# Aggregation of a graph attention layer: how far one-hot matrices are made ahead, and where they are kept

## The reference

```
z = einsum('ni,hoi->nho', h, Wfc)           # 3750 x 8 heads x 64
alpha = ex / denom[dst]                     # one coefficient per edge and head
msg = alpha[:, :, None] * z[src]
out = segment_sum(msg, dst, num_segments=N) # sum over the edges of each node
```

## Time and profile before

| | |
|---|---|
| median of 3 runs | 3725.33 us |
| profiled execution: time, span | 3727.02 us, 3724.9 us |
| TensorE, weight loads | busy 2880.1 us (77%), 1386.2 us |
| VectorE, ScalarE, GpSimd | 2141.4 us, 611.7 us, 1619.3 us |
| mean granted TensorE clock | 0.88 of full speed |
| aggregation of layer 0 | 529 to 1158 us of the span |
| aggregation of layer 1 | 2549 to 3179 us |

### The profile page before, as it was taken

One profiled execution on the slowest core, in us unless ns is written; L12 is line 12 of the kernel. 1 busy time (PEld: TensorE's weight loads), 2 busy tenths in 40 slices (PEclk: granted clock), 3 DMA queues, 4 the chain that ended last, 5 costly groups with the idle time before them and its releaser, 6 DMA issues. The chain is left out here.

```text
span 3724.9 us, 37926 instructions
## 1 busy us (share of the span) xinstructions
PE 2880.1 (77%) x9194; PEld 1386.2 (37%) x9195; DVE 2141.4 (57%) x3396; ACT 611.7 (16%) x1083; POOL 1619.3 (43%) x1595
## 2 busy tenths in 40 slices
PE   5988638988886881499998598925988887649980
PEld 2444312222223551255553244512223322546660
DVE  5779786666654876633331404587666664754445
ACT  2100110000003650011111210012111110611110
POOL 0777027777760000144443077404777775002216
PEclk9999869999997875699999799967999998559995
DMA  4336227777761211055554537404777775143337
GB/s 155 87 98 117 87 63 211 210 210 211 210 190 52 77 68 68 21 138 144 142 141 99 145 89 160 128 7 126 211 210 211 210 211 150 73 165 127 126 104 249
DMA packets 330788, 512.22 MB, mean 138 GB/s; under 512 B 172499, under 2 KB 178115, under 8 KB 329999
## 3 DMA queue, kind: packets, MB, share of 16 engines
q0 software_dynamic: 113824, 311.79, 31.4%
q1 hardware_dynamic: 92975, 194.62, 14.9%
q10 hardware_dynamic: 123840, 3.94, 1.9%
HBM read 423.29 MB, written 86.92 MB: 137 GB/s over the span
## 5 line engine op out<-in xcount | busy, mean ns | idle before, releaser
L1049 PE MATMUL bank<-aggregate_zg,aggregate_onehot 128*128 x2112 | 1085.9, 640 | 167.0 <-DVE aggregate_zg L1019 95.0
L976 POOL DMA_INDIRECT aggregate_zg<-z_rows,src_groups x940 | 889.1, 946 | 657.1 <-POOLq L2239 334.9
L1019 DVE TENSOR_TENSOR aggregate_zg<-aggregate_zg,bank 128x1024 f32<-128x1024 f32 x470 | 573.9, 1221 | 467.6 <-DMA aggregate_zg<-z_rows,src_groups 467.1
L1049 PEld LDWEIGHTS bank<-aggregate_zg,aggregate_onehot 128*128 128x128 f32 x2112 | 348.4, 193 | 903.2 <-issue 896.8
L376 POOL DMA_INDIRECT front_d<-src_scores,src_chunks x320 | 321.5, 1005 | 188.6 <-issue 97.2
L1651 POOL DMA_INDIRECT exp_xg<-hn_rows,exp_gather_tok x64 | 71.7, 1120 | 536.0 <-DVE exp_gather_tok L1713 414.8
L672 PE MATMUL bank<-front_w,front_table 128*120 128x512 bf16 x960 | 242.6, 390 | 27.7 <-DVE front_w L549 27.7
L1795 PE MATMUL bank<-exp_w,exp_h_t 128*117 128x512 f32 x512 | 225.8, 595 | 0.7 <-ACT exp_h_t L1742 0.7
L959 ACT ACTIVATE acc<-bank 128x512 f32<-128x512 f32 x60 | 35.8, 597 | 1146.6 <-PE bank L1049 1146.6
L997 DVE TENSOR_TENSOR aggregate_onehot<-bank,columns 128x256 f32<-128x256 f32 x528 | 215.6, 417 | 0.0
L1662 POOL DMA_INDIRECT x_rows<-exp_y,exp_add_tok x64 | 137.0, 2141 | 165.0 <-DVE exp_y L1704 129.8
(11 more groups left out here) (398 smaller groups left out, 3518.8 us busy)
## 6 DMA issues: line engine op xcount, KB each, us to landing
exp_w<-in_L_ffn_w SPq DMA_DIRECT2D x32, 1024.0 KB, 7.7
slot_out<-exp_y SPq DMA_DIRECT2D x66, 256.0 KB, 2.0
z_rows<-front_z SPq DMA_DIRECT2D x60, 256.0 KB, 2.0
hn_rows<-fin_xn SPq DMA_DIRECT2D x20, 768.0 KB, 3.5
aggregate_zg<-z_rows,src_groups POOLq DMA_INDIRECT x940, 3.7
front_early<-src_key SPq DMA_DIRECT2D x16, 640.0 KB, 3.9
front_early<-src_tile SPq DMA_DIRECT2D x16, 640.0 KB, 4.6
front_edge<-src_key SPq DMA_DIRECT2D x16, 640.0 KB, 4.1
```

Source lines behind the costliest of these rows:

```text
L976: pool.indirect_dma_start(zg[:, r, j, :], None, k.z_rows[:, :], bass.IndirectOffsetOnAxis(k.src_groups[:, n:n + 1], 0)).then_inc(gathered[ ...
L1019: v.tensor_tensor(z, z, bcast_last(scales[:, at:at + J * H], DH), ALU.mult).then_inc(msg_ready, 1)
L1049: mm = nc.tensor.matmul(k.banks[:, bass.ds(bank, 1), :].rearrange("p a n -> p (a n)"), onehot[:, n % RING, j, :], zg[:, bass.ds(at, 1), j, ...
```

## The change

Lookahead: `LOOK` = 22 becomes `look(g)`, which is 22 and one more for each 16 groups, at most 26 for groups below 104 and at most 30 from there on (30 from group 128 on; 28 at group 104).

Ring: 27 places serve the one-hots below number 128 as before. One-hots 128 to 134 go into seven further places, and from 135 on one-hot n goes into the place of one-hot n - 34 and waits for step n - 34. The seven places are no new memory: they are the first 1792 columns of `alpha`, the coefficients of groups 0 to 111, which by then have been copied to PSUM. The assertion states that the last of these copies stands before their first use. The comparison and the matmuls take their place from `onehot_at(n)`.

```diff
--- before.py
+++ after.py
@@ -52,6 +52,9 @@
 SLOTS = 8
 LOOK = NT - SLOTS
 RING = LOOK + 5
+WIDE = RING + 7
+WIDE_FROM = 128
+WIDE_GROUP = 104
 HD = D // 2
 GP = NG // 2
 WORD = 256
@@ -927,6 +930,22 @@
         lanes = k.banks[:, OPEN + 1, 0:P]
         scales = k.banks[:, 6:8, :].rearrange("p b n -> p (b n)")
         slot = lambda g: (g + 1) % SLOTS
+
+        def onehot_slot(n):
+            return n % RING if n < WIDE_FROM else RING + n - WIDE_FROM if n < WIDE_FROM + WIDE - RING else onehot_slot(n - WIDE)
+
+        def onehot_before(n):
+            return n - RING if n < WIDE_FROM else -1 if n < WIDE_FROM + WIDE - RING else n - WIDE
+
+        def onehot_at(n):
+            at = onehot_slot(n)
+            return onehot[:, at, :, :] if at < RING else k.alpha[:, (at - RING) * J * P:(at - RING + 1) * J * P].rearrange("p (j n) -> p j n", j=J)
+
+        def look(g):
+            return min(LOOK + g // SCALE_BLOCK, RING - 1 if g < WIDE_GROUP else NT)
+
+        extra_blocks = -(-(WIDE - RING) * J * P // (SCALE_BLOCK * J * H))
+        assert (extra_blocks - 1) * SCALE_BLOCK <= WIDE_FROM - RING
         with nc.Block() as block:
             @block.scalar
             def _(act):
@@ -992,9 +1011,9 @@
                     return v.tensor_copy(scales[:, at:at + wide], k.alpha[:, g * J * H:g * J * H + wide]).then_inc(scales_ready, 1)
 
                 def make_onehot(n):
-                    if n >= RING:
-                        dve.wait_ge(summed, n - RING + 1)
-                    v.tensor_tensor(onehot[:, n % RING, :, :], lanes.unsqueeze(1).to_broadcast([P, J, P]), bcast_last(k.columns[:, n, :], P),
+                    if onehot_before(n) >= 0:
+                        dve.wait_ge(summed, onehot_before(n) + 1)
+                    v.tensor_tensor(onehot_at(n), lanes.unsqueeze(1).to_broadcast([P, J, P]), bcast_last(k.columns[:, n, :], P),
                                     ALU.is_equal).then_inc(onehot_ready, 1)
 
                 if layer == 1:
@@ -1004,7 +1023,7 @@
                 dve.wait_ge(lanes_copied, 1)
                 made = 0
                 for g in range(NGR):
-                    upto = min(STEPS, g + min(LOOK, 3 + 3 * g))
+                    upto = min(STEPS, g + min(look(g), 3 + 3 * g))
                     for n in range(made, upto):
                         make_onehot(n)
                     made = upto
@@ -1046,7 +1065,7 @@
                     pe.wait_ge(onehot_ready, n + 1)
                     pe.wait_ge(msg_ready, group)
                     for j in range(J):
-                        mm = nc.tensor.matmul(k.banks[:, bass.ds(bank, 1), :].rearrange("p a n -> p (a n)"), onehot[:, n % RING, j, :],
+                        mm = nc.tensor.matmul(k.banks[:, bass.ds(bank, 1), :].rearrange("p a n -> p (a n)"), onehot_at(n)[:, j, :],
                                               zg[:, bass.ds(at, 1), j, :].rearrange("p a n -> p (a n)"), start=False, stop=True, skip_group_check=True)
                         if j == 0 and n + 1 < STEPS:
                             coming = word(n + 1)
```

## The result

The changed kernel takes 3657.05 us, the median of four runs (3656.24 to 3657.77). The kernel before, run beside it, takes 3724.11 us, the median of its three runs above and a fourth (3719.47 us). The ratio is 0.9824 (95% interval 0.9807 to 0.9841). The prediction was 3661 us, with a range of 3653 to 3675. The profiled execution has a span of 3654.2 us, against 3724.9.

The account below looks back on a forecast made before the run. Gather issue sets the pace until late one-hots put TensorE behind and the slots bind. Gains of 33.8 + 30.9 = 64.7 us from 3727.0 give 3662.3, or 3661 on the median's footing; range 3653 to 3675.

Parts of the forecast that it names:

- What bounds the kernel: In the aggregation, the queue that issues the gathers is full and sets the pace: 1.250 us each, 2.50 us a group.
- Why TensorE was behind: Late in each layer, from tile 22 on, one-hots come after t - 21 later multiplies, leaving TensorE seven groups behind.
- The lookahead: Late in each layer, no step waits for a one-hot any more: 33.8 us gained in layer 0, 30.9 in layer 1.
- A step back to back: At the end of the aggregation, a TensorE step without gaps costs between 1.7 and 2.0 us; both were carried.
- The places: Seven one-hot places in the copied coefficients, serving 28 of 264 steps: taken as 0, at most 0.4 us.
- The ring's wait: VectorE's wait before reusing a one-hot place stays five or more steps behind TensorE below step 128; it does not bind.
- The one-hots beside the gathers: Moving one-hots beside gathers costs nothing; were they of the barred kind, 3.3 us a layer, 6.7 us in all.
- The clock: Stays at 1.00 to the aggregation's end, else 6.4 us a layer; next stage's clock return moves 2.5 us either way.
- Only the tail goes: Rival, chance 0.05: late gathers stay as they are, only the layer ends shorten, 14.8 + 13.4 = 28 us gained: 3697.
- TensorE stays a little behind: Rival, chance 0.06: late steps keep a backlog of a few steps, gain less by up to 2 x 6.4 us: about 3674.
- the ring binds: Rival, chance 0.03: VectorE waits on the ring of 27 in groups 16 to 103, 300 us slower: about 3960.
- no effect: Rival, chance 0.01: the late one-hots are not what TensorE waits for; the kernel stays at 3725 us.

Follow-up runs that it names:

- the runs with 26 and 24: The changed kernel with its lookahead held at 26, one run of 3671.66 us, and at 24, 3672.13 us, the median of three.
- six slots: The changed kernel, but a gather waits until the group six before it is summed, not eight: one run of 3663.32 us.
- late growth only: The changed kernel with a lookahead of 22 up to group 151 and 30 from 152 on, at once: 3662.27 us, ratio 0.9846.

## Why the prediction was right

*What bounds the kernel.* The pace of the gathers, 1.250 us, held to the last, with the clock at 1.00 and one step of backlog; that it is issue and not bytes was argued from GpSimd's idle time of 0.30 us, and the run with half the bytes shows it.

*Why TensorE was behind.* Right in the mechanism, wrong by one in its count. The prediction says that a late step's one-hot comes after t - 21 later multiplies, eight in the last tile. A one-hot is made before multiply g + t - 21, so after the one of group g + t - 22: t - 22 later multiplies lie ahead of it, seven in the last tile. The trace had seven. No term of the sum used the eight. One part of the lateness has no term in it: with gaps between its steps TensorE was also slower. From 1092 to 1158 us the steps of the kernel before were not all 2.1 us long; where the granted clock was 0.67 (1130 to 1140 us) and 0.80 (1120 to 1130), single steps took 2.96 to 3.60 us. One of them:

```profile
1129.47 3.60 PE L1049 MATMUL bank<-aggregate_zg,aggregate_onehot 128*128 x4 [1.47 <-issue]
```

In the changed kernel the clock is 1.00 there. So the 19.0 us of waiting that the change took away held the late one-hots and, as their consequence, slower steps; no run separates the two.

*The lookahead.* Layer 0 gave 34.0 us (33.8 predicted), layer 1 31.3 (30.9). The last gather was put 586.4 us after the first and was 586.4; from there to the last matmul 8.1 us and it was 7.9. That the second number fits so well is in part luck. The last multiply was put 3.8 us after its gather and came after 4.4. And the ends don't follow from the terms given: four steps of 1.7 to 2.0 us from 1115.9 on end at 1122.7 to 1123.9, and not at 1123.3 to 1124.0, so by its own terms the end would have been 0.1 to 0.6 us sooner. The four steps took 7.73 us (1113.62 to 1121.35), 1.93 us each.

*A step back to back* was left between 1.7 and 2.0 us. Where nothing is waited for, four and six steps take 7.29 and 10.71 us in the runs with 26 and 24, that is 1.82 and 1.79 us each. Each further step is (10.71 - 7.29)/2 = 1.71 us. The long row of 24 matmuls in the earlier trace rows holds waits for multiplies inside it.

*The places.* Zero, as taken. The matmuls of layer 0 with their one-hot in the ring and in the coefficients:

```profile
L1068 PE MATMUL bank<-aggregate_zg,aggregate_onehot x944: 592/592/1212, 533.8 to 1120.8; 128*128 x189
...
L1068 PE MATMUL bank<-aggregate_zg,alpha x112: 592/592/692, 819.1 to 1060.2; 128*128 x112
```

The median is 592 ns in both, and the kernel without the seven places is as fast.

*The ring's wait.* It did not bind, with 34 places or with 27.

*The one-hots beside the gathers.* The gathers did not slow (586.4 us for 469, with eight more one-hots beside them). Even nine in a row, 3.06 us, left the gathers beside them at their distance of 1.25 us. The trace agrees with the Trainium skill, "SBUF — State Buffer", section "SBUF: two separate sides", in that an elementwise operation of two tensors does not hold up the building of descriptors.

*The clock* stayed at 1.00 to the end of the stage, as the step times assumed. In the next stage it came back at about the same distance from the last matmul (24 us, before some 23), within the 2.5 us taken as bound.

*The rivals.* "Only the tail goes" and its 14.8 us for a tail by itself have no footing: in the run that moves the last one-hots alone the tail lost 3.5 and 1.4 us. The tail and the gathers' waits have one cause. "TensorE stays a little behind", "the ring binds" and "no effect" did not come about: no gather waits, VectorE never waits before a one-hot, and the stages are 34.0 and 31.3 us shorter. The 4 us between forecast and result (3661 and 3657.05) are hardly in the stages, where 65.3 us stand against the 64.7 of the sum; the profiles have 5.4 us more outside them, in code that is the same.

## What to carry to other kernels

Here VectorE makes one-hots with a fixed lead counted in groups (22), and TensorE uses them up by steps. There is one step more than groups with each tile that is closed, so the lead shrinks by one with each tile: count such a lead at the end of the loop, not at its start.

Buffers and lead are one budget. The time after which a slot is wanted again (2.5 us times the slots, less 1.25) must exceed the time for which it is held (some 8.3 to 8.6 us, an estimate added up from the rows, and 2.5 us for each later multiply that the one-hot comes after). So either may look free by itself (a lead of 24, or six slots), while both together cost nearly all of the gain.

Look at how late the consumer is, by counting instructions up to a time, because the trace put these waits down to "issue" and to the engine that releases the slot, and not to the one-hot.

## What the runs showed of the hardware

Gathers of 128 rows keep 1.250 us from start to start whether a row has 2 KB or 1 KB (586.4 and 586.3 us for 469). On another chip the same instruction kept 1.253 us throughout (587.8 us), 0.003 us more for each, in two different kernels (late growth only, and six slots).

With the bytes halved the multiply of the last group starts 3.62 us after its second gather and not 4.41 us: the bytes are in the way from issue to use, though not in the pace.

A step of two matmuls of 512 columns of fp32 takes 2.1 us where each waits for its multiply; back to back each further step adds 1.71 us (7.29 us for four, 10.71 us for six). While TensorE had idle gaps of 1.5 to 3.5 us between its steps (1100 to 1140 us of the kernel before), the granted clock was 0.67 to 0.84 in windows of 10 us, and single steps took up to 3.60 us.
